# Two chained LoRA layers with a seven-product W multiplication: the residual identity moves into W's blocks, W's sums are made anew in each group, and the images lose their first-layer rows

## The reference

```
# layer 0, adapters A0 (2048 x 16), B0 (16 x 2048) of sequence n
x1 = x + (x @ B0.T) @ A0.T
# layer 1, weights W (2048 x 2048), bias b, adapters A1 (2048 x 16), B1 (16 x 2048)
out = x1 + x1 @ W.T + b + 2.0 * (x1 @ A1) @ B1
```

## Time and profile before

| | |
|---|---|
| median of 3 runs | 1411.78 us (1410.3 to 1412.83) |
| profiled execution, its time | 1409.31 us |
| its span (first to last instruction) | 1407.5 us |
| mean granted TensorE clock | 0.994 of full |
| PE, DVE, ACT busy | 98%, 69%, 34% of the span |
| moved by DMA | 320.98 MB, mean 228 GB/s |

### The profile page before, as it was taken

The page is one execution under the profiler, slowest core; times in us unless marked ns, Lnnn a source line. Parts: engine busy times, 40 slices in busy tenths (PEclk is TensorE's granted clock), DMA queues, the critical chain, the costliest instruction groups (busy, mean ns, idle before and its releaser), DMA issues.

```text
span 1407.5 us, 16133 instructions
## 1 busy us (share of the span) xinstructions
PE 1373.3 (98%) x5992; PEld 1128.7 (80%) x5992; DVE 967.0 (69%) x1015; ACT 484.7 (34%) x491; POOL 94.1 (7%) x194
## 2 busy tenths in 40 slices
PE   5999989999999999999999999999999999999999
PEld 4787778888878888888888888888888888888887
DVE  5778777786768897666646676666655766666662
ACT  3444344323223333333323343333233334332331
POOL 3013210001000000000001000000101000000000
PEclk9999999999999999999999999999999999999999
DMA  9988863798999898466757334456856444457642
GB/s 348 317 291 292 282 233 131 258 376 300 317 355 336 302 303 291 166 220 233 240 198 241 128 120 156 169 187 214 276 199 228 141 137 135 154 171 249 197 152 83
DMA packets 106094, 320.98 MB, mean 228 GB/s; under 512 B 14240, under 2 KB 15392, under 8 KB 106016
## 3 DMA queue, kind: packets, MB, share of 16 engines
q1 hardware_dynamic: 99360, 307.35, 63.8%
q0 software_dynamic: 6656, 12.60, 2.8%
HBM read 264.31 MB, written 55.57 MB: 227 GB/s over the span
## 4 chain that ended last, share of the span: by engine, by line
PE 86%; DMA 6%; DVE 4%; issue 2%; SPq 1%; ACT 1%; POOLq 0%; POOL 0%; DVEq 0%; ACTq 0%
PE acc L546 26%; PE acc L547 26%; PE acc L548 26%; PE down_ps L516 2%; PE acc L530 2%; PE down_ps L517 2%; DMA bg_raw<-w_rows 1%; DMA w_two<-w 1%; DVE bg_lo L720 1%; DMA w_sums<-w_one 1%; DVE w_one L689 1%; DVE w_lo L693 1%; DMA bg_raw<-x 1%; PE image_ps L498 1%; DMA image<-a 1%
## 5 line engine op out<-in xcount | busy, mean ns | idle before, releaser
L546 PE MATMUL acc<-x_hi,w_hi 128*128 128x512 f32 x1792 | 704.5, 393 | 18.9 <-DVE x_lo L715 13.6
L547 PE MATMUL acc<-x_lo,w_hi 128*128 128x512 f32 x1792 | 701.4, 391 | 0.0
L548 PE MATMUL acc<-x_hi,w_lo 128*128 128x512 f32 x1792 | 700.9, 391 | 0.0
L583 ACT ACTIVATE w_hi<-w_one 128x1024 fp32r<-128x1024 f32 x224 | 237.4, 1060 | 679.1 <-PE acc L548 620.2
L546 PEld LDWEIGHTS acc<-x_hi,w_hi 128*128 128x128 f32 x1792 | 338.6, 189 | 92.8 <-issue 14.0
L547 PEld LDWEIGHTS acc<-x_lo,w_hi 128*128 128x128 f32 x1792 | 338.7, 189 | 71.8 <-issue 1.0
L548 PEld LDWEIGHTS acc<-x_hi,w_lo 128*128 128x128 f32 x1792 | 338.1, 189 | 71.4
L693 DVE TENSOR_TENSOR w_lo<-w_one,w_hi 128x1024 fp32r<-128x1024 f32 x224 | 273.7, 1222 | 110.1 <-ACT w_hi L583 110.1
L758 DVE SCALAR_TENSOR_TENSOR sums<-acc,bias_sb,sums 128x512 f32<-128x512 f32 x128 | 95.7, 748 | 43.6 <-PE acc L530 43.6
L715 DVE TENSOR_TENSOR x_lo<-x_stage,x_hi 128x1024 fp32r<-128x1024 f32 x80 | 96.1, 1222 | 43.0 <-ACT x_hi L602 42.8
L602 ACT ACTIVATE x_hi<-x_stage 128x1024 fp32r<-128x1024 f32 x80 | 83.4, 1056 | 103.9 <-DVE x_stage L709 82.2
(11 more groups left out here) (54 smaller groups left out, 628.6 us busy)
## 6 DMA issues: line engine op xcount, KB each, us to landing
w_one<-w SPq DMA_DIRECT2D x128, 512.0 KB, 5.6
w_one<-w_sums SPq DMA_DIRECT2D x96, 512.0 KB, 3.2
w_two<-w SPq DMA_DIRECT2D x64, 512.0 KB, 8.0
x_stage<-x SPq DMA_DIRECT2D x64, 512.0 KB, 4.6
out<-sums SPq DMA_DIRECT2D x128, 256.0 KB, 4.4
w_sums<-w_one SPq DMA_DIRECT2D x40, 512.0 KB, 5.3
resident<-x SPq DMA_DIRECT2D x32, 512.0 KB, 7.0
sums<-x SPq DMA_DIRECT2D x64, 256.0 KB, 4.9
```

What stands on the lines that cost most here:

```text
L546: pe.matmul(ps[:, :], w_hi[ws][:, c, :], hi, start=(c == 0), stop=False)
L547: pe.matmul(ps[:, :], w_hi[ws][:, c, :], lo, start=False, stop=False)
L548: mm = pe.matmul(ps[:, :], w_lo[ws][:, c, :], hi, start=False, stop=(c == H - 1))
L583: act.activation(w_hi[s % W_PARTS][:, :, :], w_one[s % W_ONES][:, :, :], ACT.Copy).then_inc(w_hi_ready, 1)
```

## The change

- **Identity in W.** `make_w` replaces `sum_w`: in all 224 steps, after the sum if there is one, DVE adds a multiple of the identity to one 128 x 128 block of `w_one` (`W_IDENTITY`). With it the products hold the residual x. ACT's `w_hi` now waits for that (`w_made`) in every step.
- **Sums start with copies.** The x loads into `sums[2]` and the adds of x are gone. In products 0, 1 and 4 ACT copies the bank into the sum (`copy`, behind `split_w` in its program); DVE adds once in products 1, 2, 3 and 5 and not in 0 and 4. In product 4 `add_rank` waits for ACT's copy, in place of DVE's add.
- **No kept sums.** `keep_sum` and `w_sums` are gone; every group loads both blocks and makes the sum: 160 sums in place of 64.
- **Images.** The first layer's rows are no longer loaded: PE adds them with two matmuls of 128 columns for each of 16 chunks of features, against the identity. DVE's add becomes a copy from PSUM. The tile `image` is no longer one of its own: it is `b1_rows`. The block's last matmul (`end_image`) moves to the 21st matmul of the step after its last chunk (steps 8, 11, 14, 17), and DVE's copy one step later too.
- SP loads the chunks of the down products one step earlier.

```diff
+W_IDENTITY = [-1.0, 2.0, 1.0, 1.0, -1.0, 1.0, 1.0]
+COPIED = [0, 1, 4]
 SUMMED = [0, 1, 2, 4, 6]
-KEPT_IN = {0: 1, 1: 1, 2: 1, 4: 0, 6: 0}
...
-            image = sb("image", [P, T], F32, early)
+        image = b1_rows
...
-                keep_sum(s + 1)
...
-                    load_bg(z)
-                if s + 2 < STEPS:
-                    load_sum(s + 2)
+                    if z < IMAGE:
+                        load_bg(z)
+                for z in background(s + 3):
+                    if z >= IMAGE:
+                        load_bg(z)
...
             def load_rows(j):
                 cols = slice(T * j, T * (j + 1))
                 if j:
-                    pool.wait_ge(image_done, j)
+                    keep_image(j - 1)
+                    pool.wait_ge(image_stored, DMA * j)
                 for n in range(NB):
                     pool.dma_start(b1_rows[R * n:R * (n + 1), :], adapter(1, n, b1).rearrange("u r d -> (u r) d")[:, cols])\
                         .then_inc(b1_rows_loaded, DMA)
-                if j:
-                    keep_image(j - 1)
-                    pool.wait_ge(image_stored, DMA * j)
-                for n in range(NB):
-                    pool.dma_start(image[R * n:R * (n + 1), :], adapter(0, n, a0).rearrange("u r d -> (u r) d")[:, cols])\
-                        .then_inc(a0_rows_loaded, DMA)
...
+                        if c // BANKS == j:
+                            part = ps[:, P * (c % BANKS):P * (c % BANKS + 1)]
+                            pe.matmul(part, wa[0], identity_sb[:, :], start=False, stop=False)
+                            pe.matmul(part, wa[1], identity_sb[:, :], start=False, stop=False)
...
+            def end_image(j):
+                pe.wait_ge(across_ready, 1)
+                pe.wait_ge(b1_rows_loaded, NB * DMA * (j + 1))
+                pe.matmul(image_ps[j % 2][:, :], across[:, :], b1_rows[:, :],
+                          start=False, stop=True).then_inc(image_done, 1)
...
-                if i != 6:
-                    pe.wait_ge(first_added, 24 * g + 8 * (i - 3) + o + 1)
+                if i == 4:
+                    pe.wait_ge(copied, copied_before(s) + 1)
+                elif i != 6:
+                    pe.wait_ge(first_added, 16 * g + 8 * (i // 5) + o + 1)
...
+                    if c == 6 and s - 1 in IMAGE_LAST:
+                        end_image(IMAGE_LAST[s - 1])
...
-                if has_sum(s):
-                    act.wait_ge(w_summed, sums_before(s) + 1)
-                else:
-                    act.wait_ge(w_one_loaded[s % W_ONES], DMA * (s // W_ONES + 1))
+                act.wait_ge(w_made, s + 1)
...
+            def copy(s):
+                g, i, o = where(s)
+                if i not in COPIED:
+                    return
+                if i == 1:
+                    act.wait_ge(bank_free, released_before(s) + 1)
+                else:
+                    act.wait_ge(step_done, s + 1)
...
+                act.activation(sums[1 if i == 1 else 2][:, o, :], acc[s % BANKS][:, :], ACT.Copy).then_inc(copied, 1)
...
+                    dve.tensor_tensor(one[:, :, :], one[:, :, :], w_two[k % W_TWOS][:, :, :], W_SIGN[i])\
+                       .then_inc(w_summed, 1)
+                    dve.wait_ge(w_summed, k + 1)
+                dve.scalar_tensor_tensor(out=one[:, o, :], in0=f32(identity_sb[:, :]), scalar=W_IDENTITY[i],
+                                         in1=one[:, o, :], op0=ALU.mult, op1=ALU.add).then_inc(w_made, 1)
...
-                if s - 1 in IMAGE_LAST:
-                    j = IMAGE_LAST[s - 1]
+                if s - 2 in IMAGE_LAST:
+                    j = IMAGE_LAST[s - 2]
                     dve.wait_ge(image_done, j + 1)
-                    dve.wait_ge(a0_rows_loaded, NB * DMA * (j + 1))
-                    dve.tensor_tensor(image[:, :], image_ps[j % 2][:, :], image[:, :], ALU.add).then_inc(image_ready, 1)
+                    dve.tensor_copy(image[:, :], image_ps[j % 2][:, :]).then_inc(image_ready, 1)
```

More of the change, by code:

```diff
@@ L126, in has_sum, with copied_before, released_before @@
 def has_sum(s):
[L128 to L133, removed]
+    return 0 <= s < STEPS and where(s)[1] in SUMMED
+def copied_before(s):
+    return sum(where(t)[1] in COPIED for t in range(s))
+def released_before(s):
+    return sum(where(t)[1] in RELEASED for t in range(s))
 def sums_before(s):
     return sum(has_sum(t) for t in range(s))
-def kept_in_slot(s):
-    return sum(keeps_sum(t) for t in range(s % W_ONES, s + 1, W_ONES))
+SUM_STEPS = [s for s in range(STEPS) if has_sum(s)]
 def rank_number(g, i):
@@ L164, in last_staged, with build @@
     return q
-def build(nc, x, ids0, ids1, a0, a0_down, b0, w, w_rows, bias, a1, b1, mask, w_sums, images, out):
+def build(nc, x, ids0, ids1, a0_down, b0, w, w_rows, bias, a1, b1, identity, mask, images, out):
     with ExitStack() as ctx:
@@ L239, in build @@
         w_summed = sem("w_summed")
-        w_kept = [sem(f"w_kept{k}") for k in range(W_ONES)]
+        w_made = sem("w_made")
         w_hi_ready = sem("w_hi_ready")
@@ L301, in load_w @@
                     sp.wait_ge(w_ready, s - W_ONES + 1)
[L302 to L307, removed]
-                else:
-                    source = w[H * one[1] + o][:, H * one[0]:H * (one[0] + 1), :]
+                source = w[H * one[1] + o][:, H * one[0]:H * (one[0] + 1), :]
                 sp.dma_start(w_one[s % W_ONES][:, :, :], source).then_inc(w_one_loaded[s % W_ONES], DMA)
@@ L316, in load_w @@
                       .then_inc(w_two_loaded[k % W_TWOS], DMA)
[L318 to L322, removed]
             def load_resident(g, k, r):
@@ L349, in load_bg @@
                 sp.dma_start(bg_raw[k][:, :, :], source).then_inc(bg_loaded[k], DMA)
[L351 to L359, removed]
             def store(s):
@@ L380, in _ @@
             load_w(1)
-            load_sum(0)
-            load_resident(0, 0, 0)
             load_w(2)
-            load_sum(1)
-            load_resident(0, 0, 1)
+            for r in range(2):
+                load_resident(0, 0, r)
             for s in range(STEPS):
@@ L466, in _ @@
             pool.dma_start(ids_sb[:, 1, :], ids1).then_inc(ids_loaded, DMA)
+            pool.dma_start(identity_sb[:, :], identity).then_inc(identity_loaded, DMA)
             pool.wait_ge(ids_loaded, 2 * DMA)
@@ L538, in step @@
                 if s >= BANKS:
-                    pe.wait_ge(bank_free, s - BANKS + 1)
+                    before = where(s - BANKS)[1]
+                    if before in (0, 1):
+                        pe.wait_ge(copied, copied_before(s - BANKS) + 1)
+                    elif before in RELEASED:
+                        pe.wait_ge(bank_free, released_before(s - BANKS) + 1)
                 pe.wait_ge(w_ready, s + 1)
@@ L655, in _ @@
                     split_w(s + 1)
+                if s >= 1:
+                    copy(s - 1)
                 if s == 1:
```

73 lines of the change are left out of this document (35 added, 38 removed).

## The result

The changed kernel takes **1445.94 us** (median, 1445.23 to 1449.05), the kernel before 1411.91 in the same comparison: ratio **1.0247** (95% interval 1.0229 to 1.0264), slower by 34 us. Forecast were 1444 us, range 1424 to 1458. The profiled execution took 1445.23 us with a span of 1443.2, 35.7 more than before.

The account below looks back on a forecast made before the run. PE, busy 98% of the span, was taken as the bound. Terms -2.9, +0.9, +28.2, -6.4, +6.5 and +6.2 gave +32.5 on the profiled 1409.3, so 1441.8; 2.5 more for the median made 1444 us, range 1424 to 1458.

Parts of the forecast that it names:

- Main term: Image blocks: serial chain of copy, store, row issues and landing makes PE wait 6.9, 8.3 and 7.3 us; +28.2 us.
- SP's earlier load: Down chunks loaded a step earlier: counted only towards the gain where group 1 begins, with no cost of its own.
- The allowance of 2.5 us: Added at the end because the median of the runs stood 2.5 us above the profiled one.
- Start: First 50 us, bound by transfers: 1.05 MB of x blocks no longer queued ahead of the first image chunk; -2.9 us.
- Begin of group 1: Stall with slow clock, SP standing behind w_sums stores, goes: no stores left, load a step earlier; -6.4 us.
- Steady waits: Groups 1 to 3, output 4 of products 0 to 2: nine PE waits of 0.57 + 0.34 us; +6.5 us.
- Product 4: Rank matmul waits for ACT's copy behind w_hi, 0.8 us late, outputs 2 and 4 in four groups; +6.2 us.
- Small matmuls: 32 matmuls of 128 columns per image block at 0.11 us each: 0.9 us per block, 3.6 in all.
- Quick transfers: Rival: store and rows land fast in emptier queues, so the image waits nearly vanish; about 1420 us, chance 0.08.
- Starved sums: Rival: DVE waits for fresh W blocks in every group, half of 96 new sums hold PE; about 1468 us, chance 0.06.
- Faster: Rival: only relief of the queues counts, image chain hidden, lighter DVE adds cover the identity; about 1403 us, chance 0.04.
- No effect: Rival: image rows come before PE in any order and all terms cancel within 3 us; chance 0.02.

Follow-up runs that it names:

- Experiments 1 and 2: Against the changed kernel: 1 gives images 0 to 2 their own tile, 1423.91 us; 2 moves DVE's image copy to the front of its part, 1420.93 us.
- experiment 8: The changed kernel with the down chunks of group 0 loaded two steps ahead, as before the change: 1448.39 us.
- experiment 9: Changed kernel with own image tile and all order swaps, 1400.21 us; with group 0's early load back, 1402.97; instead with step 18's chunks first on DVE, 1396.75.
- experiment 3: The changed kernel, but in groups 1 to 3 DVE splits the next step's chunk ahead of the W sum and identity: 1442.44 us.
- experiment 4: Also written copy_first: the changed kernel, but in product 4 ACT copies the bank before it makes w_hi: 1439.77 us.
- experiment 6: The changed kernel with the first four x loads of 256 KB put back in SP's queue, read by nothing: 1449.23 us.
- Experiment 7: The kernel before with one part alone: W sums always made anew, 1410.77 us; or down chunks loaded a step earlier from group 1 on, 1409.03 us.

## Why the prediction was right, point by point

By its own terms, against the two spans (35.7 us apart). The last two terms and those for steps are differences in the lengths of steps, start to start:

| term | forecast | measured in the profile |
|---|---|---|
| start and block 0's small matmuls, to step 9 | -2.0 | 88.91 - 91.55 = -2.6 |
| step 9 to the first down matmul of step 19 | +28.2 | 123.8 - 97.0 = +26.8 |
| step 20 | not seen | 12.55 - 7.25 = +5.3 |
| rest of step 19 behind that matmul, and step 21 | not seen | 6.02 - 7.48 - 0.2 = -1.7 |
| begin of group 1 | -6.4 | 6.63 - 12.94 = -6.3 |
| nine waits before a down chunk | +6.5 | +7.8 |
| eight waits before the rank matmul | +6.2 | +6.4 |
| sum | +32.5 | +35.7 |

- **Main term: right in mechanism, and in its sum partly by luck.** Chains of 23, 24 and 15 us behind the copy were forecast as 21.5 each; waits of 7.7, 10.5 and 2.8 as 6.9, 8.3 and 7.3. Experiments 1 and 2 cut the chain at two places and each took the waits away, so its being serial is shown. The sum holds because the error of the third is opposite to the others'. I had 8.0 us from the store's issue to the first row issue and 4.5 for the landing; they were 9.6, 8.4 and 4.9, and 5.2, 5.9 and 1.97. The short landing is SP's stand, the short store is not (experiment 8). All three chains were given one size, although the rows had a quicker store too (6.2). (The parts' own bounds add up to 18.7 and 24.6, not quite the 18.5 and 24.8 of the forecast.)
- **The step that failed: SP's earlier load, priced at nothing.** I counted "the load is a step earlier" as a gain only, and did not ask what stands behind it in SP's queue. In group 0, where the two buffers are used by the very chunks ahead, it holds W's blocks; it cost a wait of 3.4 us with slow clock behind it in step 20, 5.3 us in all. In the medians of experiment 9 the price is about 2.8 us (1402.97 - 1400.21). The total came near because 3.7 us of other terms went the other way: 0.6 in the start, 1.4 in the stretch, and 1.7 of slow clock, which the kernel before had behind its wait in step 19 (0.57) and this execution had not (1.00 from 212 to 220). The last is luck of the execution: in experiments 3 and 4, with the same program there, PE waited 4.2 us at that place and step 19 took 13.3 us in place of 10.4. The allowance of 2.5 us from the profiled execution to the median was 0.7.
- **Start.** The bytes are shown (experiment 6: 3.3 us by the medians for 1.05 MB, forecast 3.0).
- **Begin of group 1.** Right, 6.3 us. Experiment 7 shows that taking the stores away is enough; the load's place alone would have given 3.4 in group 1.
- **Steady waits.** 0.85 listed before each down chunk where 0.91 was forecast, 0.33 for the identity row where 0.34 was. In groups 2 and 3 a step with such a wait is 1.15 us longer than before, a little more than the wait that is listed, so the term came out 1.3 high. That w_hi leads, and DVE's lost adds therefore give nothing, fits all of them.
- **Product 4.** Right: 0.74 in place of 0.8 each, between starts. ACT's order alone makes it (experiment 4).
- **Small matmuls.** Right: the starts show their price (timeline of PE, changed kernel, step 9). Half a chunk with two of them takes 91.20 - 90.29 = 0.91 us, one without them 95.52 - 94.84 = 0.68. The two cost 0.23, so 0.115 each, half of the pace, where 0.11 was taken; step 9, with four of them, is 0.49 longer than before.

```profile
90.29 0.39 PE L475 MATMUL image_ps<-bg_hi,a_hi 128*128 128x512 f32 x1
90.52 0.39 PE L476 MATMUL image_ps<-bg_hi,a_lo 128*128 128x512 f32 x1
90.74 0.22 PE L479 MATMUL image_ps<-identity_sb,a_hi 128*128 128x128 f32 x1
90.80 0.28 PE L480 MATMUL image_ps<-identity_sb,a_lo 128*128 128x128 f32 x1
90.91 0.45 PE L481 MATMUL image_ps<-bg_lo,a_hi 128*128 128x512 f32 x1
91.20 0.39 PE L475 MATMUL image_ps<-bg_hi,a_hi 128*128 128x512 f32 x1
```

- **Rivals.** Quick transfers: in part, in one chain of three, and its 15.3 us are still above the 14.6 that the rival named. The Trainium skill (DMA: Bandwidth & Descriptors, "Anatomy of one DMA — SWDGE (gpsimd) path") has 2.0 us fixed per transfer plus the bytes, from which I estimate 2.6 for a store of 256 KB and 2.1 for a row load. Here a row load took 1.97 with DMA busy 0.25 (196 to 200), which agrees, and 5.2 to 5.9 beside other traffic; the store took 3.75 us with DMA busy 0.57 (184 to 188), and 8.4 and 7.2 beside other traffic, all above the estimate. Starved sums: DVE waited for w_two 14.8 us in all, twice in the first 26 us and once at 220.85, behind SP's stand; never in the late groups. Faster: false for this kernel; the orders of experiment 9 bring its time, by other means. No effect: false, at 34 us.

What stays open: why the slow clock follows one wait of 2 to 3 us and not another, why the start differs by 2.4 us between executions, and the exact price of the earlier load.

## What to carry to other kernels

When a tile gets a second use, write down the chain that now runs through it, from who empties it to who fills it again, with the issue time of many small DMAs in it: here one shared 2 KB row per partition made 23 us out of loads that had been hidden. A load moved earlier in an in-order queue is not free: ask which buffer it waits for and what stands behind it. And when an engine off the critical path gets another consumer (ACT's copy, DVE's chunk), put what PE waits for ahead of work for two steps later; four such swaps, with the tile and the load put back, turned a loss of 2.5% into a gain of 1%. Check each swap for what it pushes back: experiment 3 lost half of its gain to the W sum that it had delayed.

## What the runs showed of the hardware

- The last of eight small row loads (32 KB each), from its issue to its landing, took 1.97 us with DMA busy 0.25 and 5.4 us with it busy 1.01, at the same place of the same program but for one load's order.
- Waits of PE add up unevenly, as the granted clock behind them differs. A wait of 2.9 us (before 212.66) was followed by granted clock 1.00, one of 3.4 us (before 223.59) by 0.60, half speed (1.2 GHz) for most of 4 us. Removing one of two neighbouring waits can leave the slow clock with the other, so a wait's price is not its length. Nor is it fixed for one program: in step 16 a wait of 2.85 us was followed by granted clock 1.00 in the changed kernel (184 to 192) and by 0.73 and 0.84 in copy_first, which has the same program there; the step took 13.62 and 14.89 us.
- Two matmuls of 128 columns with weights of their own, between matmuls of 512, add 0.23 us at clock 1.00; a 512-column one has 0.227.
